# Counting edges into the adjacency in groups of four: one PSUM bank, one signal and one wait for each group

## The reference

```python
h = relu(layernorm(x)); x = x + relational(h, bases, w_comp, h_bias, edge_weight1, src, dst, edge_type)
h = relu(layernorm(x)); x = x + gcn2(h, src, dst, W1, b1, W2, b2)
h = relu(layernorm(x)); x = x + message_passing(h, src, dst, edge_attr_20, edge_weight, edge_attr_4, ...)
h = relu(layernorm(x)); x = x + sage2(h, src, dst, W1_l, W1_r, b1, W2_l, W2_r, b2)

# relational: sum over edges of norm * (h[src] @ sum_b w_comp[type, b] * bases[b]), added up at dst
# gcn2: twice  segment_sum(dis[src] * dis[dst] * (h @ W)[src], dst) with self loops, dis = deg ** -0.5
# sage2: twice (segment_sum(h[src], dst) / deg) @ W_l.T + h @ W_r.T + b
# message_passing: gathers rows by dst, multiplies them with filters of the edge's attributes, adds up at src
```

## Time and profile before

| | us |
|---|---|
| median of 3 runs | 1467.24 |
| lowest and highest run | 1462.48, 1468.37 |
| the profiled execution, in all | 1460.51 |
| its span, first to last instruction | 1458.7 |
| busy in the span: PE, DVE, POOL, ACT | 1375.7, 865.4, 890.9, 497.0 |
| the count stage, first to last count | 457.5 to 666.6 |
| POOL's scatters end | 853.0 |
| POOL's first gather of the message steps | 859.2 |
| last product of the message steps | 1189 |

### The profile page before, as it was taken

One profiled execution on the slowest core, in us unless ns is written; L12 is line 12 of the kernel. 1 busy time (PEld: TensorE's weight loads), 2 busy tenths in 40 slices (PEclk: granted clock), 3 DMA queues, 4 the chain that ended last, 5 costly groups with the idle time before them and its releaser, 6 DMA issues. The chain is left out here.

```text
span 1458.7 us, 24667 instructions
## 1 busy us (share of the span) xinstructions
PE 1375.7 (94%) x6924; PEld 938.6 (64%) x6925; DVE 865.4 (59%) x2485; ACT 497.0 (34%) x1279; POOL 890.9 (61%) x927
## 2 busy tenths in 40 slices
PE   4888899999999999999999998999999979999998
PEld 2788888888885433344595775666665656686565
DVE  8777745555555667766343337998888854411111
ACT  7000000000005887773621235565555546311100
POOL 5777777777777777777777767777777720000000
PEclk9999899999999999999999998999999989999999
DMA  4678789878885552223121122222222230000000
GB/s 164 192 229 232 222 290 321 255 240 258 268 263 160 162 169 76 77 77 117 33 57 25 35 61 62 69 62 66 73 66 66 83 80 1 29 1 29 8 29 36
DMA packets 104170, 173.00 MB, mean 119 GB/s; under 512 B 20155, under 2 KB 54128, under 8 KB 104080
## 3 DMA queue, kind: packets, MB, share of 16 engines
q0 software_dynamic: 42832, 103.15, 24.1%
q10 hardware_dynamic: 27790, 39.30, 8.8%
q1 hardware_dynamic: 33458, 29.39, 6.5%
HBM read 153.74 MB, written 18.02 MB: 118 GB/s over the span
## 5 line engine op out<-in xcount | busy, mean ns | idle before, releaser
L873 POOL DMA_INDIRECT gath<-h_rows,idx x313 | 303.1, 968 | 96.0 <-issue 65.8
L1007 PEld LDWEIGHTS ps<-spread,gath 128*128 128x128 f32 x2504 | 313.4, 201 | 68.5 <-issue 42.4
L1007 PE MATMUL ps<-spread,gath 128*128 128x96 f32 x2504 | 315.5, 285 | 23.6 <-DMA gath<-h_rows,idx 16.2
L1029 PE MATMUL ps<-base_t,z 128*128 128x512 f32 (+1 forms) x640 | 321.8, 614 | 0.0
L929 POOL DMA_INDIRECT u<-u_rows,at x219 | 218.9, 999 | 66.7 <-issue 62.5
L1546 DVE TENSOR_TENSOR z<-z,ps 128x384 f32 x313 | 172.4, 551 | 103.7 <-PE ps L1007 91.7
L899 POOL DMA_INDIRECT slots<-att,idx_s x160 | 161.1, 1007 | 49.5 <-issue 47.6
L899 POOL DMA_INDIRECT slots<-z,idx_s x153 | 154.4, 1009 | 43.9 <-issue 40.9
L1220 PE MATMUL ps<-msg,hot 128*128 128x256 f32 x648 | 160.6, 391 | 16.2 <-DVE msg L1915 14.7
L1220 PEld LDWEIGHTS ps<-msg,hot 128*128 128x128 f32 x648 | 118.5, 191 | 75.3 <-DVE msg L1915 54.1
L612 ACT ACTIVATE z<-ps 128x512 f32<-128x512 f32 x5 | 3.0, 597 | 411.0 <-PE ps L1029 410.9
(11 more groups left out here) (297 smaller groups left out, 1902.1 us busy)
## 6 DMA issues: line engine op xcount, KB each, us to landing
base_t<-in_bases_dram ACTq DMA_DIRECT2D x116, 256.0 KB, 3.2
slots<-att SPq DMA_DIRECT2D x21, 256.0 KB
at<-slots SPq DMA_DIRECT2D x21, 256.0 KB, 2.7
gath<-h_rows,idx POOLq DMA_INDIRECT x313, 4.2
u<-u_rows,at POOLq DMA_INDIRECT x219, 2.5
att<-in_attr_dram SPq DMA_DIRECT2D x40, 64.0 KB, 2.0
slots<-att,idx_s POOLq DMA_INDIRECT x160
z<-in_attr_dram SPq DMA_DIRECT2D x39, 64.0 KB
```

Of the source, the lines that this page charges most:

```text
L873: nc.gpsimd.indirect_dma_start(out=gath[:, c % RING, :], out_offset=None, in_=h_rows, in_offset=bass.IndirectOffsetOnAxis(ap=idx[:, par, c ...
L1007: last = mm(bank[:, k * SPREAD:(k + 1) * SPREAD], gath[:, h_slot, k * P:(k + 1) * P], s_of.rearrange("p b d -> p (b d)"), start=True, stop ...
L1029: return mm(ps[BANKS[n]][0:rows(n), :], z[:, k, b, n * P:n * P + rows(n)], base_t[:, k, :], start=(t == JOINS[n]), stop=(t == JOINS[n] + T ...
```

## The change

The counts are made in groups of four. `counted` now rounds down to a multiple of four, except at the very end, so behind a product stand either no count or four; the last group brings five (chunks 308 to 311, and chunk 312, a group of its own). A group writes its four results side by side into one bank (480 columns), banks 5 and 7 by turns of groups. It waits once (for four compares, for two pairs of `hot_s`, and for the first add after the group before last), and signals `a_pe` once, on its last count.

On DVE the order changes. Before, a compare stood behind each add. Now, when a group's counts are done, the four compares of the next group come first, with one signal behind the last, and then the four adds of the group one behind the other, each still waiting for the add before. On ACT the ring of three pairs stays, with waits for whole groups.

```diff
@@ counted
-            return max(0, min(REAL_CHUNKS, (i + 1 - COUNT_FROM) * REAL_CHUNKS // COUNTED))
+            there = max(0, min(REAL_CHUNKS, (i + 1 - COUNT_FROM) * REAL_CHUNKS // COUNTED))
+            return there if there == REAL_CHUNKS else there // QUAD * QUAD
@@ source_pair
-                    act.wait_ge(a_pe, 2 * (p - PAIRS) + 2)
+                    act.wait_ge(a_pe, (p - PAIRS) // 2 + 1)
@@ the loop over the weight tiles on ACT
-                while pairs <= REAL_CHUNKS // 2 and 2 * (pairs - PAIRS) + 2 <= counted(tile_end(t - KIN + 1) - 1):
+                while pairs <= REAL_CHUNKS // 2 and ((pairs - PAIRS) // 2 + 1) * QUAD <= counted(tile_end(t - KIN + 1) - 1):
@@ count
-                pe.wait_ge(hot_ok, t + 1)
-                if t % 2 == 0:
-                    pe.wait_ge(hot_src, t // 2 + 1)
-                if t == 0:
-                    pe.wait_ge(o_free, 2)
-                if t >= 2:
-                    pe.wait_ge(a_add, t)
-                mm(ps[5 + t % 2 * 2][:, 0:AWIN], hot_s[:, t // 2 % PAIRS, t % 2, :], hot_d[:, t % QUAD, 0:AWIN], start=True, stop=True)\
-                    .then_inc(a_pe, 1)
+                g, q = t // QUAD, t % QUAD
+                if q == 0:
+                    pe.wait_ge(hot_ok, g + 1)
+                    pe.wait_ge(hot_src, min(2 * g + 2, REAL_CHUNKS // 2 + 1))
+                    if g == 0:
+                        pe.wait_ge(o_free, 2)
+                    if g >= 2:
+                        pe.wait_ge(a_add, (g - 1) * QUAD + 1)
+                last = mm(ps[5 + g % 2 * 2][:, q * AWIN:(q + 1) * AWIN], hot_s[:, t // 2 % PAIRS, t % 2, :],
+                          hot_d[:, q, 0:AWIN], start=True, stop=True)
+                if q == QUAD - 1 or t == REAL_CHUNKS - 1:
+                    last.then_inc(a_pe, 1)
@@ make_hot
-            def make_hot(t, slot):
-                v.tensor_scalar(hot_d[:, slot, 0:AWIN], iota_a[:, 0:AWIN], acol[:, bass.ds(t, 1)], None, ALU.is_equal)\
-                    .then_inc(hot_ok, 1)
+            def make_hot(t):
+                return v.tensor_scalar(hot_d[:, t % QUAD, 0:AWIN], iota_a[:, 0:AWIN], acol[:, bass.ds(t, 1)], None, ALU.is_equal)
@@ count_oct
-                    dve.wait_ge(a_pe, t + 1)
+                    if q % QUAD == 0:
+                        dve.wait_ge(a_pe, t // QUAD + 1)
+                        further = range(t + QUAD, min(t + 2 * QUAD, REAL_CHUNKS))
+                        for n in further:
+                            last = make_hot(n)
+                        if further:
+                            last.then_inc(hot_ok, 1)
                     dve.wait_ge(a_add, t + 1)
                     cw = cnt[:, :, bass.ds(w[q], WIN)]
-                    v.tensor_tensor(cw, cw, ps[5 + q % 2 * 2][:, 0:AWIN].rearrange("p (d s) -> p s d", s=BLOCKS), ALU.add)\
-                        .then_inc(a_add, 1)
-                    if q < further:
-                        make_hot(t + QUAD, q % QUAD)
+                    v.tensor_tensor(cw, cw, ps[5 + t // QUAD % 2 * 2][:, q % QUAD * AWIN:(q % QUAD + 1) * AWIN]
+                                    .rearrange("p (d s) -> p s d", s=BLOCKS), ALU.add).then_inc(a_add, 1)
@@ the start of the stage on DVE
                 for t in range(QUAD):
-                    make_hot(t, t)
+                    last = make_hot(t)
+                last.then_inc(hot_ok, 1)
```

7 lines of the change are left out of this document (3 added, 4 removed).

## The result

The changed kernel takes **1457.39 us** in the median of the runs, the kernel before, run beside it, 1466.33: a ratio of 0.995, with a 95% interval of 0.9934 to 0.9965. One of its five runs was slow (2297.45 us at a granted clock of 0.56) and is left out of the ratio. A second comparison (h1_changed, the same code) gives 1456.55 against 1463.82, 0.9962 (0.9945 to 0.9979). So it is faster by 7 to 9 us, where 1482.7 was forecast. The two profiled executions differ by less, 1456.16 against 1460.51 (spans 1454.3 and 1458.7). The profile puts these waits down to no other engine (in g1 "issue", 316.7 us of TensorE's in 20 waits); that they are waits for its own code is my reading, and the text calls them so.

A forecast was written before the change was run, and what follows sets the result against it. TensorE set the count stage's pace before, DVE's cycle would after: 459.7 + 77 x 2.77 + 5 + 3.5 = 681.5, TensorE leaving near 682 against 666.65; time 1467.24 + 15.5 = 1482.7 us, range 1463 to 1494.

The forecast's parts named there:

- TensorE's side: Count stage: 124 fewer changes between products and counts gain 6.2 us, 12.8 without short stalls; 2.51 us for each group.
- DVE's new cycle: Count stage, first compare to the next group's first: 2.77 us, ends 2.70 and 2.84, against TensorE's 2.51.
- four compares and the way to the first add: In DVE's cycle: compares 0.224 us apart, three times, 0.67; then 0.25 from the last compare to the first add.
- the three waits from add to add: In DVE's cycle, between a group's four adds: three at 0.48 us, 1.44 in all.
- rival 1: Count stage: chained adds are cheap, cycle 1.93 us, TensorE leaves 12.8 us sooner, 4 to 8 remain, time 1461; chance 0.12.
- the 0.20 to the next compare: In DVE's cycle: 0.20 us from the last add to the next group's first compare.
- The load: Load of eight windows between last add and compare on DVE: about 0.4 us for two groups, 0.2 each.
- `take_low`: Fifteen parts on DVE's path in the count stage, 0.35 us each, 5 us in all (5 to 7).
- An add that waits for its predecessor costs 0.20, and the compare lay in that hole for nothing: DVE's count stage: 0.20 us idle before each chained add, which hid the compare before the change.
- A delay is paid in full, a gain is not.: Behind the count stage: TensorE's delay moves gathers and message steps by as much; gathers can't start before slots are read back.
- The degrees: Behind the count stage: ready some 10 us behind TensorE's exit, asked for 13.8 us behind it; no cost.
- The clock: Rival 3, count stage: DVE's pace idles TensorE 10%, the granted clock falls to 0.88, time 1491; chance 0.03.

The follow-up runs named there:

- g1: The changed kernel without the last 9 of POOL's 313 scatters, in a run with TensorE waiting for its code; ratio 0.9908 to the kernel before.
- e1: The changed kernel with two waits before each add, where it had one in three cases of four; ratio 0.9976 to the kernel before.
- f2: The changed kernel with four waits before each add, three of them long reached; ratio 0.9987 to the kernel before.
- e2: The changed kernel with a signal behind each compare, TensorE waiting for the fourth; ratio 0.9913 to the kernel before.
- j3: The changed kernel with two waits before each add and an unused windows load at each group's head; 1457.15 us, 0.9964 to the kernel before.
- k1: The changed kernel with two waits before each add and each add in two halves, run only with the wait for code; 1.0102 to the kernel before.

## Why the prediction was wrong

**TensorE's side was right.** 0.05 for a change and 0.06 for a count make 0.29 for a group; measured 0.26 to 0.27. The stage without stalls was put at 196.4 us; it took 197.6 (457.82 to 655.40) with 4 us of stalls, so 193 without.

**The step that failed is DVE's new cycle**, 2.77 us forecast with ends of 2.70 and 2.84, 2.32 measured:
- four compares and the way to the first add: 0.67 + 0.25 forecast, 0.65 measured. This was a misreading. The row is merged; its 0.92 less one compare, divided by three, gave 0.224, but the four start 0.16 apart there as everywhere, and the fourth lasts 0.44. The trace of the kernel before shows this when the four are listed one by one.
- the three waits from add to add: 1.44 forecast, 1.23 measured. The 0.48 of the earlier trace rows was right for an add with two waits, and the change drops one in three cases of four. The text named this in rival 1, but as all or nothing (0.20 or 0.48 from add to add); it is a part, 0.07 of it.
- the 0.20 to the next compare was right. The load costs 0.47 for two groups, 0.24 each, where 0.20 was taken. `take_low` moves an add or a compare by 0.38 to 0.41 (0.35 forecast), but at 2.32 against 2.51 it has room.

That is 2.77 - 0.27 - 0.21 + 0.04, up to rounding. The first two put DVE below TensorE's 2.51 instead of above, and the sign turned. Rival 1 had this outcome, with adds 0.20 apart and a cycle of 1.93 that did not come. The ends were too narrow as well: they spanned 0.14 us, with TensorE's 2.51 just 0.19 below, though no row showed an add with one wait. The experiments show how near that is, by their pace: e1's one further wait costs some 6 us of the exit's 11, f2's four all of it.

**"An add that waits for its predecessor costs 0.20, and the compare lay in that hole for nothing"** was right in kind: 0.41 without and 0.42 with a compare between. The idle part of it is 0.13 with one wait; the 0.20 has the instruction for the second wait in it., which the prediction held against rival 1, are both adds with two waits and that instruction in front, the one of the edge stage too (at 208.54, between the add that ends at 208.50 and the one at 208.70), so they could not tell what an add with one wait costs. The Trainium skill (VectorE: DVE Perf Modes, The DRAIN you can't avoid) says that a semaphore behind each operation costs nothing extra. e2 agrees for signals (0.73 with one or four); for waits the runs disagree: two cost 0.07 more than one, and four 0.10 more.

**"A delay is paid in full, a gain is not."** The second half was right, and so was rival 1 on it: POOL near 857.5 (856.38, in h1 858.13), no stop for `u_rows`, 4.4 us left at the end (4.2). Of its 4 to 8 us for the whole, 4.4 came in the profiled executions, 7.3 in the second comparison and 8.9 in the first, so its time, 1461, is 4 us above the 1457.4 measured. j3 shows the same from the other side: between the new exit and the old one, 7.3 us at TensorE are 2.6 us at the last step. The first half speaks of exits later than the old one; no undisturbed run made such a one, and k1 only speaks for it.

**The rest.** The degrees were hidden, as forecast (`sum_blocks` starts at 657.95, the degrees 13.8 us behind the exit). The clock did not fall in the stage (1.00). The range's lower end, 1463, was too high since only a part of rival 1, at 0.12, was taken into it.

## What to carry to other kernels

Count the waits in front of an instruction, not only its work: in this chain of short VectorE operations the second wait is 15% of the step, and dropping it by grouping was, by e1's pace, worth about half of what the change gains on TensorE. Before a spacing is taken from a merged row, list its instructions one by one: one long instruction at its end looks like a wider spacing. Where two engines meet in a cycle, look at the place of the operand that the other waits for, and not at the cycle's length alone. And where a later engine works through a list at its own pace, ask for both signs how much of a shift its list covers.

## What the hardware showed beyond that

- Waits already reached are not always free on DVE: 0.41 us from add to add with one, 0.48 with two, 0.51 with four. A further wait is an instruction of 0.02 us in DVE's queue (0.05 with two waits in it). It costs when it has to pass between the end of an add and the next (0.07), and nothing when it passes while the add before still runs. Whether exchanging the two waits would make the second one free was not tried.
- Independent compares of 0.247 us start 0.16 apart, in the middle of the stage and at its start alike; of the four at the start the last lasts 0.43 to 0.44 in all twenty traces.
- An indirect scatter of 32 rows takes POOL 0.86 us, one of 128 rows 0.97: most of its price does not depend on the rows.
- The granted clock fell behind the second convolution to 0.50, the level of 1.2 GHz, in all six undisturbed traces, after a stretch in which TensorE was less busy (3.26 of the 5 us from 855 in the changed kernel). It came back at different times, even in the same kernel: for 875 to 880 it was 0.94 in the changed kernel's first profile and 0.55 in h1; in the kernel before it was 0.50 for 875 to 885. How much of the scatter between executions comes from this is not shown.
